# A relational message-passing kernel: TensorE's order in a pair is regrouped into three runs, and the sort gets a second PSUM bank

## The reference

```python
# x (6250, 64) f32; src, dst, edge_type (200000,) i32, sorted by dst; weight (16, 64, 64)
h = jnp.maximum(_layernorm(x, axis=-1), 0.0)
h_src = h[src]
for r in range(16):
    mask = edge_type == r
    msg = msg + h_src * mask[:, None] @ weight[r]
out = x + segment_sum(msg, dst, num_segments=6250)
```

## Time and profile before

| | |
|---|---|
| three runs | 1197.76, 1200.71, 1206.26 us |
| profiled execution, span | 1203.7 us; the page gives no other time of it |
| TensorE busy | 1083.9 us, 90%, 15421 matmuls |
| VectorE busy | 938.3 us, 78% |
| GpSimd busy | 682.1 us, 57% |
| ScalarE busy | 450.0 us, 37% |
| granted TensorE clock | 0.984 of 2.4 GHz in the mean |

### The profile page before, as it was taken

How to read it: one execution, slowest core, us unless ns; L and a number is a source line. 1 busy time by engine, 2 the same in 40 slices (tenths; PEclk the granted TensorE clock), 3 DMA queues, 4 the chain that set the end, 5 groups by cost and what they waited for, 6 DMA issues and landing times.

```text
span 1203.7 us, 39145 instructions
## 1 busy us (share of the span) xinstructions
PE 1083.9 (90%) x15421; PEld 740.5 (62%) x15421; DVE 938.3 (78%) x2773; ACT 450.0 (37%) x1157; POOL 682.1 (57%) x647
## 2 busy tenths in 40 slices
PE   3998999899989889999999999999999999999897
PEld 1445666666666566666666666666666666666665
DVE  7756878897877688788778778878887887888874
ACT  4884333333333333333333333333333333333332
POOL 2213665566666665667666666666665656666630
PEclk9998999999999899999999999999999999999999
DMA  6795222222222122222222122222222222222211
GB/s 173 301 401 186 59 61 59 58 59 59 62 59 59 37 57 59 59 60 58 59 58 57 43 59 58 60 59 58 60 59 60 59 58 59 58 60 59 59 32 56
DMA packets 41739, 93.69 MB, mean 78 GB/s; under 512 B 14572, under 2 KB 14574, under 8 KB 41557
## 3 DMA queue, kind: packets, MB, share of 16 engines
q1 hardware_dynamic: 13850, 42.12, 10.3%
q0 software_dynamic: 19776, 20.29, 9.9%
q10 hardware_dynamic: 7930, 28.76, 6.2%
HBM read 63.52 MB, written 27.59 MB: 76 GB/s over the span
## 4 chain that ended last, share of the span: by engine, by line
PE 74%; issue 8%; DVE 6%; ACT 5%; another core or an unknown queue 3%; DMA 2%; ACTq 1%; POOL 0%; SPq 0%; DVEq 0%; POOLq 0%
PE ps L1281 33%; PE ps L1264 21%; PE ps L1308 6%; PE ps L1324 3%; ACT u L602 3%; PE ps L1173 3%; DVE u L946 2%; PE ps L1164 2%; PE ps L1197 2%; DMA table<-u 1%; DMA w_cat<-weight 1%; PE ps L1158 1%; PE ps L1203 1%; PE ps L1186 1%
## 5 line engine op out<-in xcount | busy, mean ns | idle before, releaser
L529 POOL DMA_INDIRECT u<-table,row_idx x583 | 612.7, 1051 | 411.3 <-PE ps L1264 138.8
L1281 PE MATMUL ps<-u 64*64 64x512 bf16 (+1 forms) x7280 | 466.5, 377 | 18.0 <-issue 16.0
L672 ACT CAST u<-ps 128x384 bf16<-128x384 f32 (+1 forms) x630 | 265.2, 465 | 527.8 <-PE ps L1264 464.2
L946 DVE TENSOR_SCALAR u<-iota_key,z_sb 128x512 bf16<-128x512 f16 x1190 | 359.9, 368 | 70.3 <-PE ps L1281 50.9
L1264 PE MATMUL ps<-parts,u 128*128 128x192 bf16 x3430 | 333.6, 250 | 11.0 <-issue 9.3
L1281 PEld LDWEIGHTS ps<-u 64*64 64x64 bf16 x7280 | 215.0, 106 | 204.7 <-issue 75.9
L1264 PEld LDWEIGHTS ps<-parts,u 128*128 128x128 bf16 x3430 | 280.6, 99 | 41.0 <-issue 38.5
L936 DVE TENSOR_SCALAR u<-u,node_id 128x1152 bf16<-128x1152 f16 (+2 forms) x420 | 184.5, 495 | 0.0
L681 ACT COPY u<-ps 128x512 f32<-128x512 f32 x140 | 75.2, 589 | 109.5 <-remote 76.8
L966 DVE TENSOR_TENSOR accT<-accT,ps 128x32 f32 x238 | 44.8, 188 | 58.4 <-DVE accT L966 23.1
L1308 PE MATMUL ps<-u,w_cat 128*64 128x128 f32 x1120 | 77.4, 277 | 1.7 <-ACT u L681 1.2
(11 more groups left out here) (131 smaller groups left out, 656.4 us busy)
## 6 DMA issues: line engine op xcount, KB each, us to landing
u<-rel_dram SPq DMA_DIRECT2D x70, 544.0 KB
table<-u ACTq DMA_DIRECT2D x24, 1024.0 KB, 5.2
u<-table,row_idx POOLq DMA_INDIRECT x583
rel_dram<-rel_row SPq DMA_DIRECT2D x70, 4.2 KB
x_sb<-x SPq DMA_DIRECT2D x2, 448.0 KB
out<-h_sb SPq DMA_DIRECT2D x3, 224.0 KB
out<-h_sb ACTq DMA_DIRECT2D x3, 224.0 KB
msg_x<-table,spill_row POOLq DMA_INDIRECT x35
```

The lines of the kernel that those rows point to most:

```text
L529: pool.indirect_dma_start(out=msg_p[:, b, j, :], out_offset=None, in_=table, in_offset=bass.IndirectOffsetOnAxis(ap=row_idx[:, j, m:m + 1] ...
L672: act.copy(msg_s[:, u % MB, 0:width, :].rearrange("p q c -> p (q c)"), ps[gather_bank(u)][:, 0:width * ROW]).then_inc(s_gev, 1)
L946: dve.tensor_scalar(khot[:, v % KR, :], iota_key[:, :], z_sb[:, n % 3, 1, q:q + 1], None, ALU.is_equal).then_inc(s_khot, 1)
L1281: last = pe.matmul(ps[3 + a][half * D:(half + 1) * D, keys], msg_s[rows, u % MB, q % 2, part * D:(part + 1) * D], khot[rows, v % KR, keys] ...
```

## The change

- TensorE does each pair in one list: gather 1, `sort_permute` (pair + 2), gather 2, `sort_ranks` (+ 3), gather 3, `rank_spilled` and `sort_turn` (+ 2); then the gathered sums of the pair, `weigh` in even pairs, `permute_spilled` (+ 1); then all sums of this same pair.
- The sort from pair 2 on uses bank 5 for z, spill ranks and the turn, and bank 6 for ranks and spilled rows. The target sums keep bank 7 alone; `weigh` and `sum_gathered` wait for the adds of the batch before instead of two before.
- ScalarE takes the first sum bank of a pair ahead of the next pair's messages and the second behind them. VectorE's list follows the new order. The time model, and so the places of fetches and gathered sums, is made anew.

```diff
-    sum_at = (0, 0, 1, 2)
+    sorted_before = 2
+    # permuted(n): n + 2, ranked(n): n + 3, spilled(n): n + 1
...
-    def target_bank(k):
-        return ps[(7, 5)[k % 2]]
+    def sort_bank(g):
+        return ps[6 if g < sorted_before else 5]
...
-            for n, c in STREAM:
-                take_messages(n, c)
-                if turned(n, c):
-                    take_rel(turned(n, c))
...
-                if c == 0 and n >= 1:
-                    take_sums(n - 1)
-                if permuted(n, c):
-                    take_z(permuted(n, c))
+            for n in range(NPR):
+                if n >= 1:
+                    take_sum(n - 1, 0)
+                take_messages(n, 0)
+                if permuted(n):
+                    take_z(permuted(n))
...
+                take_messages(n, 1)
+                take_messages(n, 2)
+                if n >= 1:
+                    take_sum(n - 1, 1)
+                if permuted(n):
+                    take_rel(permuted(n))
+                if spilled(n) and spilled(n) % 2 == 1:
+                    take_spilled(spilled(n))
...
             for n in range(NPR):
+                key_hots(n, KEYS_EARLY, SQ)          # KEYS_EARLY = 6
+                for m in sums_in[n]:
+                    gathered_hots(m)
+                if ranked(n):
+                    sort_slots(ranked(n))
+                    sort_values(ranked(n))
...
+                if permuted(n):
+                    sort_spilled(permuted(n))
+                    source_hots(n + 1, 0)
+                if n % 2 == 1 and 3 <= n < NPR - 1:
+                    add_sums(n // 2)
+                    source_hots(n + 1, 1)
...
+                    key_hots(n + 1, 0, KEYS_EARLY)
...
             def permute_spilled(g):
-                pe.wait_ge(s_relrow, g + 1)
-                if g >= 2:
+                if g < sorted_before:
+                    pe.wait_ge(s_relrow, g + 1)
+                else:
+                    pe.wait_ge(s_slots, min(g + 3, NPR))
                     pe.wait_ge(s_xzev, g // 2)
...
             def weigh(g):
-                    pe.wait_ge(s_add, added_by(k - 2))
+                    pe.wait_ge(s_add, added_by(k - 1))
...
-            for i, (n, c) in enumerate(STREAM):
-                gather(n, c)
-                if turned(n, c):
-                    rank_spilled(turned(n, c))
-                    sort_turn(turned(n, c))
-                if spilled(n, c):
-                    permute_spilled(spilled(n, c))
...
-                if i:
-                    sum_sorted(*STREAM[i - 1])
-                for m, at in zip(sums_in[n], sum_at):
-                    if c == at:
-                        sum_gathered(m)
-                if permuted(n, c):
-                    sort_permute(permuted(n, c))
-                if ranked(n, c):
-                    sort_ranks(ranked(n, c))
-                if n >= 2 and n % 2 == 0 and c == weigh_at:
-                    weigh(n // 2 - 1)
+            for n in range(NPR):
+                gather(n, 0)
+                if permuted(n):
+                    sort_permute(permuted(n))
...
+                gather(n, 1)
+                if ranked(n):
+                    sort_ranks(ranked(n))
+                gather(n, 2)
+                if permuted(n):
+                    rank_spilled(permuted(n))
+                    sort_turn(permuted(n))
+                for m in sums_in[n]:
+                    sum_gathered(m)
+                if weighed(n) is not None:
+                    weigh(weighed(n))
+                if spilled(n):
+                    permute_spilled(spilled(n))
+                for c in range(len(CHUNKS)):
+                    sum_sorted(n, c)
```

More of the change, by code:

```diff
@@ L84, in gnn_program, with permuted, ranked, spilled @@
     CHUNKS = ((0, 3), (3, 6), (6, GB))
-    STREAM = [(n, c) for n in range(NPR) for c in range(len(CHUNKS))]
-    weigh_at = 1
-    sum_at = (0, 0, 1, 2)
-    def sort_pair(n, c, ahead, at):
-        return n + ahead if n + ahead < NPR and c == at else None
-    permuted = lambda n, c: sort_pair(n, c, 2, 0)
-    turned = lambda n, c: sort_pair(n, c, 2, 1)
-    spilled = lambda n, c: sort_pair(n, c, 2, 2)
-    ranked = lambda n, c: sort_pair(n, c, 3, 2)
+    SUMS_MOST = 4
+    sorted_before = 2
+    def permuted(n):
+        return n + 2 if n + 2 < NPR else None
+    def ranked(n):
+        return n + 3 if n + 3 < NPR else None
+    def spilled(n):
+        return n + 1 if sorted_before <= n + 1 < NPR else None
+    weighed = lambda n: n // 2 - 1 if n >= 2 and n % 2 == 0 else None
     def banks_of(n, c):
@@ L186, in gnn_program @@
             tile_time.append(max(at, spots[go]))
-    place = [min(n for n in range(NPR) if starts[n] >= tile_time[before(m) + len(tiles_of(m)) - 1] + 1.4 + LANDED or n == NPR - 1)
+    place = [min(n for n in range(2, NPR) if gathered_at[n] >= tile_time[before(m) + len(tiles_of(m)) - 1] + 1.4 + LANDED or n == NPR - 1)
              for m in range(NP)]
@@ L204, in sum_place @@
         return slice(at, at + PW)
[L206 removed]
+    assert GR == 4 and GR * SW + max(len(ms) for ms in batches) * PW <= BANK and max(len(ms) for ms in sums_in) <= SUMS_MOST and not batches[0]
     assert 128 + 2 * SJ * NSB <= 448
@@ L965, in add @@
                     here = accT[rows, bass.ds(base, width)]
-                    dve.tensor_tensor(here, here, bank[rows, at], ALU.add).then_inc(s_add, 1)
+                    dve.tensor_tensor(here, here, target[rows, at], ALU.add).then_inc(s_add, 1)
                     added[0] += 1
@@ L1307, in weigh @@
                     half, first = r % 2, r < 2
-                    last = pe.matmul(target_bank(k)[half * D:(half + 1) * D, 0:GR * SW], w_cat[:, r, :], agg[:, :, r * SW:(r + 1) * SW],
+                    last = pe.matmul(target[half * D:(half + 1) * D, 0:GR * SW], w_cat[:, r, :], agg[:, :, r * SW:(r + 1) * SW],
                                      start=first, stop=r >= R - 2)
@@ L1312, in weigh @@
                     if r == R // 2 - 1:
-                        pe.matmul(target_bank(k)[0:D, 0:GR * SW], msg_x[:, g % 2, :], win_x[:, g % 2, :], start=False, stop=False)
+                        pe.matmul(target[0:D, 0:GR * SW], msg_x[:, g % 2, :], win_x[:, g % 2, :], start=False, stop=False)
                 last.then_inc(s_fl, 1)
```

138 lines of the change are left out of this document (64 added, 74 removed).

## The result

The changed kernel takes 1264.8 us (median of 4 runs, 1258.8 to 1268.7), the kernel before, in runs alternated with it, 1201.2 (1197.8 to 1206.3): a ratio of 1.052, interval 1.049 to 1.055. The prediction was 1146 us, range 1085 to 1200. The profiled execution of the changed kernel has a span of 1262.6 us against 1203.7 before: 58.9 us, or 58.9 / 68 = 0.87 us more for each pair, where 0.85 less was forecast. The other 0.19 comes from the pairs before and behind this stretch.

The account below looks back on a forecast made before the run. The prediction took TensorE, busy 90% of the span, as the bound. Per pair 0.60 + 0.50 + 0 - 0.25 = 0.85 us gained, x 68 = 58 us off 1203.7, gave 1146 us, range 1085 to 1200.

Parts of the forecast that it names:

- a: TensorE's changes of tiling fall from a mean of 8.5 to 3 per pair, at 0.11 us each: 0.60 us gained.
- b: TensorE's waits before permutation (for VectorE) and spill ranks (for ScalarE) lose their cause: 0.50 us per pair gained, bounds 0 to 0.7.
- c: TensorE's short stalls without a releaser stay as they are: 0 us per pair, bounds +0.5 and -0.7.
- d: New TensorE waits in the gather run, weighing and spilled permutation: 0.25 us per pair lost, bounds 0 and 2.4.
- (1): Nine banks gathered in one run through three PSUM banks wait for ScalarE's copies: 0.15 us per pair lost.
- (2): The weighing, directly behind the gather run, waits for ScalarE to take the second sum bank: 0.05 us per pair lost.
- (3): The spilled permutation waits for VectorE's slots of pair n+3: 0.05 us per pair lost.
- The slower rival: Gather run waits for ScalarE's late copies, 2.4 us per affected pair; at 70% of pairs 1241 us; chance 0.10.
- single target bank: Rival: weighing and gathered sums wait for VectorE's adds, 2.6 us in two pairs, giving 1234 us; chance 0.02.
- VectorE as the bound: Rival: TensorE's waits and stalls shrink until VectorE limits at 13.5 us per pair, 1055 us; chance 0.12 for 1055 to 1100.

Follow-up runs that it names:

- prompt sets: Sets of runs in which the unchanged kernel before took 1064 to 1066 us and ScalarE starts 0.69 us after a gather run starts.
- the kernel before with the deeper ring: Kernel before with VectorE's ring of key masks 30 deep instead of 22: 1062.8 us beside 1064.4, ratio 0.999.
- messages first: Changed kernel, but ScalarE copies a pair's first three message banks ahead of the previous pair's first sum bank: 1085.8 us (1.019) in one set, 1257.9 (1.054) in another.
- late traces: Traces from sets in which the unchanged kernel before took 1178 to 1201 us; those of the result, before and changed, are of this kind.
- masks first: Changed kernel with sums between all gather chunks again, next pair's first source masks ahead of the slots, spilled rows' masks behind the second half: 1207.2 us (1.026); elsewhere 1077.7 (1.012).
- the control: Changed kernel with four small matmuls per pair in the sums' own 64x64 tiling, adding no change of tiling: 1082.3 us beside 1064.4, ratio 1.017.

## Why the prediction was wrong

In us per pair of the two 800 us windows, TensorE's busy time went from 14.45 to 13.95, 0.50 gained, and its idle time from 1.26 to 2.43, 1.18 lost: together the 0.68 by which a pair is longer there.

**a held, and part of it was paid back in clock.** The traces have 435 changes of tiling in the window before and 146 after, 8.5 and 3.0 per pair, as counted. In the prompt sets TensorE's busy time fell from 1008.5 (the kernel before with the deeper ring) to 970.8 (messages first, its page): 37.7 / 70 = 0.54 us per pair, beside 0.60 forecast. In the window of the late traces 0.50 shows, at a lower clock. The mean granted clock of the span fell from 0.984 to 0.965. As it has two levels, 1.2 and 2.4 GHz, the lower one held 2 x 0.016 x 1203.7 = 39 us before and 2 x 0.035 x 1262.6 = 88 after; 50 us more at half speed cost up to 25. Of these, 27 lie in the window (20 and 48 us there), up to 14 us or 0.28 per pair; the rest, up to 11 us, can be most of what the change lost outside it. The prediction had no term for it. That the new waits bring it is argued, from one row: the clock came back to 1.00 in the window of masks first, where most of them were gone.

**b held, at the lower of its values.** The 20.6 us of waits for ScalarE and VectorE before the permutation and the spill ranks are gone: 0.40 per pair, beside 0.50.

**c failed.** It priced the stalls without a releaser at nothing gained or lost, as "the same matmuls and weight loads are issued". Before, they were 39 us in 800: 25.8 in the earlier trace rows and the 12.9 of the gathered sums, here beside their group:

```profile
L1324 PE MATMUL ps<-u 128*64 128x32 f32 x876 | 44.4, 226 | 13.1 <-issue 12.9
```

After, the groups above have 66 (9.9 + 30.0 + 3.1 + 3.0 + 16.5 + 2.8 and small ones). Some 8 of these are a wait that the profile doesn't name. Six times in the window the spilled permutation starts 0.1 us after VectorE's slots end, which is the wait that the change adds. VectorE and TensorE, changed kernel:

```profile
483.89 1.09 DVE L821 TENSOR_TENSOR u<-iota_slot,rank 128x896 f16<-128x896 f16 x1
...
485.08 0.51 PE L1212 MATMUL ps<-vals,spill_hot 128*64 128x8 f16 x7 [1.43 <-issue]
```

That leaves 58 us: 0.77 to 1.19 per pair, 0.42 lost, inside the bound of -0.7 but not at the value taken. In the prompt profile of messages first the gathers and the sums have no idle time at all. So these stalls aren't a property of the matmuls, as c took for granted; they come in the sets where reports are late.

**d is the step that decided.** Idle time with a cause, outside b, went from 64.0 - 39 - 20.6 = 4.4 us in 800 to 118.7 - 58 = 61: 1.25 - 0.09 = 1.16 lost per pair, where 0.25 was taken and 0 to 2.4 was the range. By its parts: (1) the gather run's waits for ScalarE 27.0 us, 0.55 against 0.15; (2) the weighing 14.5, 0.30 against 0.05; (3) the slots before the spilled permutation 8, 0.16 against 0.05; and the sums' wait for ScalarE's first sum bank 5.9, 0.12, which had no term. (The changed kernel's trace from its second set has 32.5, 17.9, 2.0 and 8.4 us: the first two parts stand, the third varies.) What the small value of (1) rested on was copies that mostly start promptly. They didn't: the first came 1.64 us behind the start of a gather run in the median of the trace of before, and 0.69 only in prompt sets.

+0.50 + 0.40 - 0.42 - 1.16 = -0.68, the 0.68 of the window.

**The slower rival was the right one**, at 1241 us with a chance of 0.10. The rows for it were all there. What weighed against it was that "the late copies follow a burst of short matmuls (ranks)", while at the kernel's end the eviction behind 68 sums began at once. That was one case, at a place where nothing follows on TensorE. In the steady state of the changed kernel the eviction begins 1.42 us behind the end of the 104 sums in the median, 1.47 behind the shorter sum runs of before; a long run of sums made the reports no prompter. "What makes it wrong is above all late reports between TensorE and ScalarE" was right.

The **single target bank** cost nothing that shows: no wait of the weighing or of the gathered sums is for VectorE's adds. The Trainium skill's rule ("Perfetto Trace Analysis", Optimizing Tensor Performance, Matmuls) that groups should rotate through banks so that evacuation overlaps was weighed against the wrong buffer. At the gather run the groups do rotate, through three banks, and it wasn't enough in a late set: the evacuation of a bank was up to 2.3 us away.

**VectorE as the bound** came true, but not by this change: in the prompt sets it is busy 186 of 200 us, in the kernel before with the deeper ring as in the edited ones. There the edited kernels are 1.2 to 2.5% slower than before, although all of them but the one with eight more changes of tiling keep TensorE busy for less time. VectorE's 2773 instructions take 955.6 us in the control and 936.3 in the kernel before with the deeper ring, and the 19.3 between them is near the difference of the spans (18.8, of 1080.0 and 1061.2). Between 300 and 1000 us, three groups are longer in the control: the mask `win_x` for the spilled rows takes 478 ns against 285 (35 in the kernel, 7 us), a key mask 383 against 377 (1190, 7 us) and a source mask 498 against 492 (420, 2.5 us). Why the same instructions take longer there is open.

No version here beats the kernel before in either kind of set.

## What to carry to other kernels

Before taking work out from between a producer's groups, look at how late the consumer starts in the steady state, not at the end of the kernel: a copy that starts 2 us after its data was made, on an idle engine, means that the work in between is a cover and must be priced as one. Idle time without a releaser isn't fixed to its instructions; where late starts and such stalls appear together, bound both as one term that can grow with the change. Each engine's list that the change reorders is a term of its own: of the 2.8 points won back here 0.9 came with the sums between the gathers and 1.9 with VectorE's list. And time the kernel before again before comparing: here it took 1065 us in one set and 1178 or more in another.

## What the runs showed of the hardware

- The kernel before took 1064 to 1066 us in three sets and 1178 to 1201 in the five others, with no change in the program. Beside each other, the traces differ in when TensorE's completions reach the other engines: ScalarE's first message copy 0.69 us after the gathers' start in the median in one kind, 1.64 in the other, with message copies 1.46 us apart that wait for banks made 0.5 us apart. TensorE's own stream pauses in the late kind: 61 to 164 places of over 0.25 us within runs of one matmul in 700 us, none in the prompt kind. Nothing here tells what makes a set late; the number of the chip doesn't, as on number 3 one set was late (1196.6 us) and another, 45 minutes later, prompt (1065.1). The Trainium skill ("Perfetto Trace Analysis", Tensor Engine Instruction (MATMUL, LD_WEIGHTS)) puts the acknowledgement by PSUM and the propagation of the semaphore behind the end that the profile shows, which is itself an estimate; it gives no time for them, and these rows measure them here only together with TensorE's pauses.
- A change between tilings of the array costs 0.10 us, mean of eight per pair in a running stream of matmuls.
